# Reading roots, convolution taps, tangents and logarithms from the PSUM bank they were made in, in a twelve-sublayer kernel with five interleaved strands

## The chip, the cores and the metric

The kernel runs on one core of one Trainium2 chip. The metric is device time in microseconds (us) for one execution of the whole program; lower is better. Engines are named as the profile names them: PE is TensorE's matmuls and PEld its weight loads, DVE is VectorE, ACT is ScalarE, POOL is GpSimd, and SP is SyncE, which here only issues transfers. SBUF is the large on-chip memory. PSUM is the small one of eight banks of 128x512 f32 into which PE writes.

## The reference, cut to what matters

Eight sequences of 512 tokens with 128 channels each pass through twelve sublayers. The ones that matter here are the layer norm ahead of every sublayer and the two-directional state-space layer ("Mamba").

```python
def _layernorm(x, axis=-1, eps=1e-05):
    m = jnp.mean(x, axis=axis, keepdims=True)
    v = jnp.var(x, axis=axis, keepdims=True)
    return (x - m) / jnp.sqrt(v + eps)
...
            xz = jnp.einsum('bld,ed->ble', x, in_proj)
            xi, z = jnp.split(xz, 2, axis=-1)
...
            xc = jax.lax.conv_general_dilated(xc, conv_w, (1,), [(D_CONV - 1, 0)], dimension_numbers=('NCH', 'OIH', 'NCH'), feature_group_count=D_INNER)
            xc = xc + conv_b[None, :, None]
            xi = jax.nn.silu(jnp.transpose(xc, (0, 2, 1)))
            dbc = jnp.einsum('bld,ed->ble', xi, x_proj)
            dt, Bm, Cm = jnp.split(dbc, [DT_RANK, DT_RANK + D_STATE], axis=-1)
            dt = jax.nn.softplus(jnp.einsum('blr,dr->bld', dt, dt_w) + dt_b)
...
                h = a * h + bx
```

The state-space layer has 256 inner channels (two groups of 128, called g = 0 and 1), a causal convolution of 4 taps, and 16 states per channel. It runs once forward ("f") and once on the reversed sequence ("b"). The other sublayers are a gated feed-forward with token shift, a small gated recurrence, a capacity router, two softmax attentions with 16 heads, a 16-expert and an 8-expert mixture.

## The kernel before, in words

Data lie with channels on the partitions and the 512 tokens of one sequence ("batch" b, 0 to 7) along the free axis, so one tile is 128x512 f32. The work is cut into five strands, each a fixed sequence of jobs:

- **L** (bank PL): the first sublayers and the preparation of the attentions (jobs `ffn0`, `att0`, `l1`, `prep`).
- **M** (bank PM): the state-space layer outside its recurrence. `lnm` is its norm, `pre` the input projection, convolution, silu and softplus, `post` the gate and output projection, `fin` the closing norm.
- **S** (bank PS): the recurrence itself, 8 batches x 2 directions x 16 states = 256 steps. A step is two scans of 128x512 on DVE (line 1194, decays made by ACT in line 1487 and inputs by POOL in line 1543), a product with the output row (line 1532 on POOL for even states, line 1200 on DVE for odd ones) and an addition to the running output (line 1173).
- **F** (two banks) the mixtures and routers, **A** (three banks) the attentions (on DVE mostly the maxima of line 1115).

Every engine runs its instructions in one fixed order. `ORDER` holds for each engine a string such as `L16M1L1M10`: take 16 pieces of strand L, one of M, and so on, where a piece ends at each `yield` of the strand's generator. `weave` executes it. A semaphore per strand and engine counts finished pieces; `j.act("rs")` is the count at which ACT has made piece "rs" of job j. A waiting instruction holds up all that stand behind it on its engine.

A layer norm `ln1` is: PE centres into the bank ("cen"); ACT copies the centred values to an SBUF tile (hA or hM, line 1254) and their squares to rL or rM (line 1256); PE averages the squares into the same bank ("avg"); ACT takes Ln of the bank into rL (line 1244) and Exp of rL into rL (line 1248), which is the reciprocal root; DVE multiplies hA by rL (line 867, "h"). There are 48 such norms with hA and 8 with hM.

A job `pre` (16 in all, `mf` and `mb` of each batch) is: PE "in0" into PM, ACT copy to tM[0] (line 1320, "cp0"), PE "in1" into PM, ACT copy to tM[1] ("cp1"); DVE for both groups in turn the first tap (line 978, "c00", "c01") and the three others (line 981) from tM into du; ACT tanh of du into xi (line 1325, "si"); DVE (xi + 1) x du (line 986, "xs"); PE "xp" into PM from both groups of xi; ACT copy (line 1329, "pj"); then per group PE "dt", ACT Abs of PM (line 1334), DVE max(PM + bias, 0) into dt (line 991, "mx"), ACT Exp and Ln in tM (lines 1338, 1342), DVE dt + tM (line 996, "dt"). PE's "dt1" waits for "mx0". POOL then forms du = dt x xi (line 1518), on which the strand S of that direction waits, and DVE scales xi (line 1000).

```python
                for d in range(4):
                    for g in range(2):
                        c, x = du[p][:, g, :], tM[:, g, :]
```

Of the kernel before, what the change touches and what calls it, by code (L numbers as in the profile page):

```python
# [40 lines left out]
for _g in GROUPS:  # L41
    _at = EDGE[-1]
    for _n, _r, _c in _g:
# [18 lines left out]
    "pe": (
        "L23M1L1M1L1M1L1M1L2M1L1M1L1M2L1M1L3M3L1M2L5M1L6M1L1M1L1M2L3M1L1M1L1M2L1M1L3M3F1M1F1M1F21L1F3M1F2M1F3M1F6M1L1M1"
        "L8A1L1A2L1A1L1A2M1L1A1L3A1M1L1M1A1L1A3M3A1M1A1M1A7M2A1L1A1M1A1L1A2L1A1M1A1M1A1L1A1L1F1A1M1F1A1L1M1F3A1L1F2L1F1"
        "L1A1F2A7F1A2F2L1F1A2F2A1F1A2F2A2F1A2F2A2F1A2F2A2F1A2F2A2F1A2F2A2F3A4F2A4F1A2L1A2L1A4M1A2L1A2L1A2L1A2M1A6L1A1M1"
        "L1A1F1L1F1A1L1A1F2A1L1F1A1F2A1L1F1A1L1F2A4F1A1L1F2A1L1F1A1F2A1L1F1A1L1F2A1F1A1F2A1M1F1A1F2A1F1A1F2A1M1F2A2F1A1"
        "F1A1F1A2M1F1A1M2F1A1M1A1F1M1A1F2A1F3A1F1A2F1A1F1A2L1A3L1A2L1A2L1A2L1A2L1A2M1A1L1A5M1A2L1A4M1A10L1A18M1A5M1L1A1"
        "L1M1A1L1M1A2M1A3F1A1M1F1A1L1M1A1F2A1L1A1F1A1F1A1F1A1F1A1L1A1F1A1F1A3F1A1L1F1A1F1A1L1A1L1F1A1F1A1F1A1F1A1F1A1F2"
        "A1L1A1F2A1F1A1F6A1F2A2F1A2F2A2F2A6F1A2L1A2F1L1A2F1A14M1L1A2L1A2L1A2F2A2M1A10L1A2M1A2L1A6L1A2L1A2L1F1A1F2A1F1A1"
        "L1F2A1L1F1A1M1F2A1L1A1F1A1F2A1L1F1A1M1F2A1F1A1F2A1L1F1A1L1F2A1F1A1F2A1F2A2F1A1F1A1F1A1M1A1F1A1M2F1A1F1A4F1A1F1"  # L70
        "A1F1A1F5A1L1F1L1A1F1M1A2L1A4L1A4L1A2L1A2L1A2F1M1A14L1A2L1A8F1A4F1A12L1A2M1A2M1A2L1M1F1A1L1F2A1F2M1A1F1A1F1A1F1"
        "M1L1A1L1A2M1A1L1A3M1A1L1M1A2L1F1A1L1F1A1M1A2F2A1M1A1F1A1F1A1F1A1F1A1L1A1F2A1F1A1F2A1F1A1F2A1F1A1F2A1F1A1F2A1F4"
        "A1F2A1F1A3F2A2F1A2F2A2F2A6F1A2L1A2F1L1A2F1A10M1L2A2L1A2F2A2M1A8L1A4M1A2L1A10L1A1L1F4A1L1F2A1F1A1L1F2A1L1F1A1F2"
        "A1L1F1A1L1F2A1F1A1F2A1F1A1L1F2A1L1F1A1F2A1F2A1M1F1A1F1A1F1A1M1A2F1A1F1A1F1A2M1A1M1A1F1M1A1F1A1F1A1F1A1F1A1F1A1"
        "F1A1F1L1F1L1A1F1L1F1L1A1M1A2L1A2L1A2L1A2M1A2F1A14F1A2L1A6L1A8F1A16M1A2M1A2L1A1M1A1F1A1L1A1L1A1F1M1A1M1F3A2F1A1"
        "M1F1M1A1L1M1A1L1A3F1A1M1F1A1L1M1A1F2A2F1A1F1A1L1F1A1F1A1L1A1L1A1F2A1F1A1F2A1L1F1A1F1A1F1A1F1A1F1A1F1A1F1A1F2A1"
        "F1A1F6A1F2A2F1A2F2A2F2A6F1A2L1A2F1L1A2F1A12M1L1A2L1F2L1M1A10L1A8L1A2M1F1A2F1A2F1A2F1A2F1A1F1A1F1A1F2A2F1A1L1F2"
# [1683 lines left out]
```

## Time and profile before

| | |
|---|---|
| median of 3 runs | 3591.86 us (3588.16 to 3598.7) |
| profiled execution, its own time | 3590.76 us |
| its span, first to last instruction | 3589.0 us |
| mean granted clock of PE | 0.781 of full speed |
| busy, share of the span | PE 76%, DVE 73%, ACT 47%, POOL 47% |

The page of the profile gives busy time by engine, the chain of waits that ended last (which engine was being waited for at each moment, followed back from the end), and groups of instructions by line. "Busy" is not "late": an engine that is busy half the time may still be waited for at every step, and one that is busy three quarters of it may be waited for seldom. The span has three parts: until 124 us no scan runs, from there to about 2932 us the 256 steps of strand S run amid the rest, and after it only mixtures and attentions are left.

### The profile page before, as it was taken

To read this page: it belongs to the slowest core of one execution; us is meant where nothing else is said; L and a number is where in the kernel's file an instruction comes from. 1 tells how busy PE (TensorE), PEld (TensorE's weight loads), DVE (VectorE), ACT (ScalarE), POOL (GpSimd) and SP (SyncE) were. 2 spreads that over 40 slices of the span, in tenths; PEclk is the share of its full clock that TensorE was granted. 3 is DMA by queue.
4 is the path that set the end of the run, shared out by engine and by line. 5 is a ranking of instruction groups with operands and counts; after the bars stand their busy time and mean duration, and the time that the engine had idled before them with its cause. 6 is when DMAs were issued, how large, how long until landed. Compare 5 with 4: busy or idle time off the path is not lost.

```text
span 3589.0 us, 31663 instructions
## 1 busy us (share of the span) xinstructions
PE 2713.3 (76%) x8594; PEld 871.9 (24%) x8594; DVE 2618.9 (73%) x3818; ACT 1682.7 (47%) x2908; POOL 1696.2 (47%) x1349
## 2 busy tenths in 40 slices
PE   5405565888888887788779787888878777987887
PEld 1101122223222222223222222222222222232222
DVE  1687888878898888788878798778868775344351
ACT  3424444563636464364537373555436261532333
POOL 1486676464736465554725464556545551121101
PEclk6656566788879987798879886887679786988768
DMA  1121122131312232222312231223212220111101
GB/s 76 57 88 63 62 96 79 50 102 53 101 46 87 72 107 68 64 82 73 114 41 83 76 103 45 79 81 99 82 61 82 76 92 25 51 56 44 44 26 38
DMA packets 158881, 253.22 MB, mean 71 GB/s; under 512 B 18928, under 2 KB 56688, under 8 KB 158448
## 3 DMA queue, kind: packets, MB, share of 16 engines
q1 hardware_dynamic: 158704, 251.18, 21.8%
q8 instruction: 72, 1.18, 0.1%
q14 instruction: 105, 0.86, 0.1%
HBM read 233.81 MB, written 16.52 MB: 70 GB/s over the span
## 4 chain that ended last, share of the span: by engine, by line
PE 39%; DVE 28%; issue 11%; ACT 9%; DMA 6%; POOL 5%; SPq 3%; DVEq 0%; POOLq 0%; ACTq 0%
PE ps L466 39%; DVE rh L1194 6%; DVE nmx L1115 5%; DMA cr<-shares 4%; DVE xib L1173 3%; ACT ps L1487 2%; DVE xif L1173 2%; SPq L1642 2%; DMA Qs<-cTN 2%; ACT tN L1434 2%; POOL rb L1543 1%; POOL tF L1557 1%; DVE rh L1200 1%; DVE hA L867 1%; ACT L1231 1%
## 5 line engine op out<-in xcount | busy, mean ns | idle before, releaser
L1194 DVE TENSOR_TENSOR_SCAN rh<-ps,rb 128x512 f32<-128x512 f32 x512 | 622.9, 1217 | 105.8 <-ACT ps L1487 102.5
L1115 DVE TENSOR_REDUCE nmx<-ps 128x1 f32<-128x512 f32 (+3 forms) x1024 | 550.2, 583 | 147.9 <-PE ps L466 146.5
L1434 ACT ACTIVATE tN<-ps 128x512 f32<-128x512 f32 (+3 forms) x1024 | 473.8, 515 | 238.2 <-PE ps L466 234.8
L1532 POOL TENSOR_TENSOR rh<-rh,cs 128x512 f32<-128x512 f32 x256 | 391.1, 1532 | 378.4 <-DVE rh L1194 377.8
L466 PE MATMUL ps<-tN,strip 128*64 128x512 f32 (+3 forms) x2048 | 507.6, 574 | 10.1 <-DVE hN L1133 7.2
L466 PE MATMUL ps<-hF,W 128*128 128x512 f32 x592 | 395.4, 755 | 96.3 <-DVE tF L1055 44.4
L1543 POOL TENSOR_TENSOR rb<-duf,bs 128x512 f32<-128x512 f32 x256 | 386.4, 1527 | 115.9 <-DVE rh L1194 110.7
L466 PE MATMUL ps<-tF,W 128*128 128x512 f32 x544 | 353.5, 745 | 89.2 <-POOL tF L1557 71.1
L1543 POOL TENSOR_TENSOR rb<-dub,bs 128x512 f32<-128x512 f32 x256 | 379.1, 1500 | 76.2 <-DVE rh L1194 65.7
L1557 POOL TENSOR_TENSOR tF<-tF,cr 128x512 f32<-128x512 f32 x128 | 172.6, 1348 | 486.7 <-DMA cr<-shares 436.2
L466 PE MATMUL ps<-Ks,Qs 48*128 48x512 bf16 (+3 forms) x1024 | 291.2, 435 | 76.0 <-DVE nmx L1115 69.6
L466 PE MATMUL ps<-Qs,Ks 51*128 51x512 bf16 (+3 forms) x1024 | 231.7, 367 | 106.6 <-ACT tN L1434 52.3
L1487 ACT ACTIVATE ps<-dtb,Am 128x512 f32<-128x512 f32 x256 | 176.8, 691 | 261.5 <-DVE rh L1194 260.0
L1576 POOL COPY strip<-V 128x32 f32<-128x32 f32 x256 | 82.8, 355 | 441.9 <-PE ps L466 439.9
L1487 ACT ACTIVATE ps<-dtf,Am 128x512 f32<-128x512 f32 x256 | 177.1, 692 | 169.4 <-DVE rh L1194 168.9
L1563 POOL TENSOR_TENSOR tF<-hF,cr 128x512 f32<-128x512 f32 x128 | 177.9, 1406 | 124.2 <-DMA cr<-shares 105.0
L1369 ACT ACTIVATE tF<-ps 128x512 f32<-128x512 f32 x144 | 85.8, 596 | 312.8 <-PE ps L466 312.5
L466 PE MATMUL ps<-X,W 128*128 128x512 f32 x192 | 145.0, 855 | 96.1 <-POOL X L1510 39.6
L1173 DVE TENSOR_TENSOR xib<-xib,rh 128x1024 f32<-128x1024 f32 x128 | 198.9, 1554 | 0.3
L1173 DVE TENSOR_TENSOR xif<-xif,rh 128x1024 f32<-128x1024 f32 x128 | 194.3, 1518 | 3.7 <-POOL rh L1532 3.5
L466 PEld LDWEIGHTS ps<-Ks,Qs 48*128 48x128 bf16 x1024 | 64.6, 97 | 530.1 <-DVE nmx L1115 347.6
L466 PEld LDWEIGHTS ps<-Qs,Ks 51*128 51x128 bf16 x1024 | 63.9, 94 | 515.9 <-ACT tN L1434 286.0
(240 smaller groups left out, 3928.0 us busy)
## 6 DMA issues: line engine op xcount, KB each, us to landing
cr<-shares SPq DMA_DIRECT2D x256, 256.0 KB
bs<-rowsf SPq DMA_DIRECT2D x128, 256.0 KB, 3.6
cs<-rowsf SPq DMA_DIRECT2D x128, 256.0 KB, 3.3
bs<-rowsb SPq DMA_DIRECT2D x128, 256.0 KB, 3.7
cs<-rowsb SPq DMA_DIRECT2D x128, 256.0 KB, 3.3
parts<-spl SPq DMA_DIRECT2D x32, 384.0 KB, 2.6
Qs<-parts SPq DMA_DIRECT2D x384, 32.0 KB
Ks<-parts SPq DMA_DIRECT2D x384, 32.0 KB
```

Source lines behind the costliest of these rows:

```text
L466: return eng.matmul(o, l, r, start=start, stop=stop, skip_group_check=skip_group_check)
L1115: red(nmx[:, qt, 8 * a + i:8 * a + i + 1], PA[u % 3][:, 0:nk], AX.X, ALU.max, negate=True).then_inc(s_red, 1)
L1173: tt(xi[p][:, :, :], xi[p][:, :, :], rh[n % NH][:, :, :], ALU.add).then_inc(s_y, 1)
L1194: eng.tensor_tensor_scan(rh[n % NH][:, g, :], PS, rb[n % NBB][:, g, :], 0.0, ALU.mult, ALU.add).then_inc(s_h, 1)
L1369: act(tF[u % NG][:, :], PF[1], ACT.Tanh).then_inc(*F.by_act(j, f"si{u}"))
L1434: act(tN[e % NP][:, q0:T], PA[a][:, 0:T - q0], ACT.Exp).then_inc(s_ex, 1)
L1487: act(PS, dt[p][:, g, :], ACT.Exp, scale=Am[:, at:at + 1]).then_inc(s_a, 1)
L1532: tt(h, h, cs[n % NB][:, :], ALU.mult).then_inc(s_cp, 1)
L1543: tt(rb[n % NBB][:, g, :], du[p][:, g, :], bs[n % NB][:, :], ALU.mult).then_inc(s_bp, 1)
L1557: tt(t, t, cr[n % NC][:, :], ALU.mult).then_inc(*F.by_pool(j, f"w{i}"))
L1563: tt(t, hF[:, :], cr[n % NC][:, :], ALU.mult).then_inc(*F.by_pool(j, f"w{i}"))
L1576: eng.tensor_copy(strips[2 * (p % 2) + a][:, :, 24:32], V9[n % 2][:, :, 8 * a + 4 * g + p, :]).then_inc(s_strip, 1)
```

## The change

Four kinds of intermediate results stay in the PSUM bank in which their inputs were made, and DVE reads them there:

- the reciprocal root of `ln1` and of `fin`: ACT's Ln and Exp write PL or PM instead of rL or rM, and DVE multiplies by the bank;
- the taps: ACT's two copies per `pre` (32 in all) are gone, and DVE's four tap instructions of a group read PM;
- the tangent of `pre` is written to PM, and "xs" reads it there;
- the logarithm of `pre` is written to PM, and DVE adds it from there.

As PM is one bank, the two groups of `pre` now go one after the other: "in1" waits for "xs0" instead of "cp0"; both matmuls of "xp" wait for "xs1"; "dt1" waits for "dt0" instead of "mx0"; and ACT's Ln of group g waits for "mx". ACT's piece with the decays' constants gets a `yield` of its own. The strings of `ORDER` for all engines are new. Of these strings the diff shows one line of PE's.

```diff
-        "L23M1L1M1L1M1L1M1L2M1L1M1L1M2L1M1L3M3L1M2L5M1L6M1L1M1L1M2L3M1L1M1L1M2L1M1L3M3F1M1F1M21L1F3M1F2M1F3M1F6M1L1M1"
+        "L23M1L1M1L1M1L2M1L1M1L1M1L1M1L2M1L2M4L1M2L9M1L2M1L1M1L1M1L1M1L2M1L1M1L1M1L2M1L2M4L1F1M1F3M1F6M1F1M1F5M1F21L2M1"
...
                 for m in range(2):
                     if m:
-                        eng.wait_ge(*j.act("cp0"))
+                        eng.wait_ge(*j.dve("xs0"))
                     mm(PM, w(f"m{p}_in", m * 128, m * 128 + 128), h[:, :]).then_inc(*M.by_pe(j, f"in{m}"))
                     yield
                 for g in range(2):
-                    eng.wait_ge(*j.dve(f"xs{g}"))
+                    eng.wait_ge(*j.dve("xs1"))
...
                 for g in range(2):
                     if g:
-                        eng.wait_ge(*j.dve("mx0"))
+                        eng.wait_ge(*j.dve("dt0"))
...
-            def ln1(j, o, r):
+            def ln1(j, o, P):
                 eng.wait_ge(*j.act("rs"))
-                tt(o, o, r[:, :], ALU.mult).then_inc(*j.strand.by_dve(j, "h"))
+                tt(o, o, P, ALU.mult).then_inc(*j.strand.by_dve(j, "h"))
...
-                for d in range(4):
-                    for g in range(2):
-                        c, x = du[p][:, g, :], tM[:, g, :]
...
                 for g in range(2):
+                    c = du[p][:, g, :]
+                    eng.wait_ge(*j.pe(f"in{g}"))
+                    ts(c, PM, cw[:, 4 * g + 3:4 * g + 4], w(f"m{p}_cb", g, g + 1), ALU.mult, ALU.add).then_inc(
+                        *M.by_dve(j, f"c0{g}"))
+                    yield
+                    for d in range(1, 4):
+                        eng.wait_ge(*j.dve(f"c{d - 1}{g}"))
+                        stt(c[:, d:], PM[:, 0:T - d], cw[:, 4 * g + 3 - d:4 * g + 4 - d], c[:, d:], ALU.mult,
+                            ALU.add).then_inc(*M.by_dve(j, f"c{d}{g}"))
+                        yield
                     eng.wait_ge(*j.act(f"si{g}"))
-                    stt(xi[p][:, g, :], xi[p][:, g, :], 1.0, du[p][:, g, :], ALU.add, ALU.mult).then_inc(
-                        *M.by_dve(j, f"xs{g}"))
+                    stt(xi[p][:, g, :], PM, 1.0, c, ALU.add, ALU.mult).then_inc(*M.by_dve(j, f"xs{g}"))
...
-                    tt(dt[p][:, g, :], dt[p][:, g, :], tM[:, 1 + g, :], ALU.add).then_inc(*M.by_dve(j, f"dt{g}"))
+                    tt(dt[p][:, g, :], dt[p][:, g, :], PM, ALU.add).then_inc(*M.by_dve(j, f"dt{g}"))
...
-                act(r[:, :], r[:, :], ACT.Exp, scale=-0.5).then_inc(*k.by_act(j, rs))
+                act(r, r, ACT.Exp, scale=-0.5).then_inc(*k.by_act(j, rs))
...
-                yield from root(j, P, r, e5, "avg", "ln", "rs")
+                yield from root(j, P, P, e5, "avg", "ln", "rs")
...
             def pre(j, p):
-                for m in range(2):
-                    eng.wait_ge(*j.pe(f"in{m}"))
-                    act(tM[:, m, :], PM, ACT.Copy).then_inc(*M.by_act(j, f"cp{m}"))
-                    yield
...
-                    act(xi[p][:, g, :], du[p][:, g, :], ACT.Tanh).then_inc(
-                        *M.by_act(j, f"si{g}"))
+                    act(PM, du[p][:, g, :], ACT.Tanh).then_inc(*M.by_act(j, f"si{g}"))
...
                     eng.wait_ge(*j.act(f"ex{g}"))
-                    act(a, a, ACT.Ln, bias=one).then_inc(*M.by_act(j, f"ln{g}"))
+                    eng.wait_ge(*j.dve(f"mx{g}"))
+                    act(PM, a, ACT.Ln, bias=one).then_inc(*M.by_act(j, f"ln{g}"))
```

On DVE, at the first `pre` of the program (batch 0, forward), there stands before:

```order
L858 TENSOR_SCALAR Am<-Am 128x64
L978 TENSOR_SCALAR duf<-tM,W 128x512 x2
L981 SCALAR_TENSOR_TENSOR duf<-tM,W,duf 128x511 x2
L981 SCALAR_TENSOR_TENSOR duf<-tM,W,duf 128x510 x2
L981 SCALAR_TENSOR_TENSOR duf<-tM,W,duf 128x509 x2
L986 SCALAR_TENSOR_TENSOR xif<-xif,duf 128x512 x2
L873 SCALAR_TENSOR_TENSOR tL<-tL,ps 128x512
```

In the changed kernel DVE has at the same place:

```order
L858 TENSOR_SCALAR Am<-Am 128x64
L976 TENSOR_SCALAR duf<-ps,W 128x512
L981 SCALAR_TENSOR_TENSOR duf<-ps,W,duf 128x511
L981 SCALAR_TENSOR_TENSOR duf<-ps,W,duf 128x510
L981 SCALAR_TENSOR_TENSOR duf<-ps,W,duf 128x509
L985 SCALAR_TENSOR_TENSOR xif<-ps,duf 128x512
L976 TENSOR_SCALAR duf<-ps,W 128x512
L981 SCALAR_TENSOR_TENSOR duf<-ps,W,duf 128x511
L981 SCALAR_TENSOR_TENSOR duf<-ps,W,duf 128x510
L981 SCALAR_TENSOR_TENSOR duf<-ps,W,duf 128x509
L873 SCALAR_TENSOR_TENSOR tL<-tL,ps 128x512
```

The taps were taken in pairs, one of each group; now all four and the tangent's product ("xs0") of group 0 precede those of group 1, and `W` stands for the pointer to the tap's weights.

On PE, at the backward `pre` of batch 3, "in0" and "in1" are the rows that read `rev`, the reversed norm. `Ks,Qs` and `Qs,Ks` are scores of the attentions, `tN,strip` their values, `hF,W` and `tF,W` the mixtures. Before, one stands four rows behind the other:

```order
L466 MATMUL ps<-rM,W 128x512
L466 MATMUL ps<-Ks,Qs 128x512 x6
L466 MATMUL ps<-X,W 128x512
L466 MATMUL ps<-Ks,Qs 128x512 x2
L466 MATMUL ps<-rev,W 128x512
L466 MATMUL ps<-rF,W 128x512
L466 MATMUL ps<-Ks,Qs 128x512 x2
L466 MATMUL ps<-X,W 128x512
L466 MATMUL ps<-rev,W 128x512
```

In the changed kernel "in0" stands 72 rows ahead of "in1", of which the last ones and the rows behind it are:

```order
L466 MATMUL ps<-hF,W 128x512
L466 MATMUL ps<-tF,W 128x512
L466 MATMUL ps<-Qs,Ks 128x512 x2
L466 MATMUL ps<-tN,strip 64x512 x2
L466 MATMUL ps<-rev,W 128x512
L466 MATMUL ps<-Qs,Ks 128x512 x2
L466 MATMUL ps<-tF,W 128x512
L466 MATMUL ps<-tN,strip 64x512 x2
```

So "in1" moved behind a good part of a mixture and the end of an attention's first phase. Over the program ACT has 154 table loads in the changed order, where it had 146.

## Rows read from the trace of the kernel before

**Rows 1.** The page: span, busy time (share of the span) and instructions by engine.
```profile
span 3589.0 us, 31663 instructions
PE 2713.3 (76%) x8594; PEld 871.9 (24%) x8594; DVE 2618.9 (73%) x3818; ACT 1682.7 (47%) x2908; POOL 1696.2 (47%) x1349
```

**Rows 2.** Two windows: length, PE, PEld, DVE, ACT, POOL busy, PE's granted clock.
```profile
124.00:500.00 376.00, 153.89 (x254) 50.78 (x255) 314.45 (x307) 151.76 (x224) 266.35 (x162) 0.57 0.22 73
500.00:2932.00 2432.00, 1949.79 (x6525) 638.72 (x6523) 2008.18 (x2871) 1251.71 (x2193) 1315.57 (x1038) 0.81 0.25 78
```

**Rows 3.** The page: chain that ended last, share by engine.
```profile
PE 39%; DVE 28%; issue 11%; ACT 9%; DMA 6%; POOL 5%; SPq 3%; DVEq 0%; POOLq 0%; ACTq 0%
```

**Rows 4.** Groups by line, DVE: busy us, mean ns | idle before.
```profile
L981 DVE SCALAR_TENSOR_TENSOR dub<-tM,W,dub 128x511 f32<-128x511 f32 (+2 forms) x48 | 51.7, 1111 | 0.0
L867 DVE TENSOR_TENSOR hA<-hA,rL 128x512 f32<-128x512 f32 x48 | 51.5, 1074 | 57.8 <-ACT rL L1248 57.8
L981 DVE SCALAR_TENSOR_TENSOR duf<-tM,W,duf 128x511 f32<-128x511 f32 (+2 forms) x48 | 44.2, 969 | 0.0
L986 DVE SCALAR_TENSOR_TENSOR xif<-xif,duf 128x512 f32<-128x512 f32 x16 | 16.4, 1039 | 1.1 <-ACT xif L1325 1.1
L996 DVE TENSOR_TENSOR dtb<-dtb,tM 128x512 f32<-128x512 f32 x16 | 14.5, 906 | 2.1 <-ACT tM L1342 1.9
L996 DVE TENSOR_TENSOR dtf<-dtf,tM 128x512 f32<-128x512 f32 x16 | 13.6, 852 | 6.7 <-ACT tM L1342 6.7
L978 DVE TENSOR_SCALAR dub<-tM,W 128x512 f32<-128x512 f32 x16 | 13.3, 847 | 0.0
L978 DVE TENSOR_SCALAR duf<-tM,W 128x512 f32<-128x512 f32 x16 | 10.3, 656 | 2.6 <-ACT tM L1320 2.6
L991 DVE TENSOR_SCALAR dtf<-ps,W 128x512 f32<-128x512 f32 x16 | 11.8, 739 | 15.7 <-ACT tM L1334 15.7
```

**Rows 5.** Single lines, durations ns min/median/max, first and last start.
```profile
L867 DVE TENSOR_TENSOR hA<-hA,rL x48: 658/693/1779, 15.0 to 3372.1; 128x512 f32<-128x512 f32 x48
L862 DVE TENSOR_TENSOR hF<-ps,rF x40: 658/682/692, 405.3 to 3558.6; 128x512 f32<-128x512 f32 x40
L1532 POOL TENSOR_TENSOR rh<-rh,cs x256: 1253/1274/2419, 132.0 to 2931.0; 128x512 f32<-128x512 f32 x128
L1173 DVE TENSOR_TENSOR xif<-xif,rh x128: 1187/1218/3366, 141.0 to 2781.9; 128x1024 f32<-128x1024 f32 x128
```

**Rows 6.** Groups by line, ACT, and one of POOL: busy us, mean ns | idle before.
```profile
L1231 ACT ACT_TABLE_LOAD x145 | 186.0, 1283 | 2.5
L1320 ACT ACTIVATE tM<-ps 128x512 f32<-128x512 f32 x32 | 18.9, 592 | 12.6 <-PE ps L466 12.6
L1532 POOL TENSOR_TENSOR rh<-rh,cs 128x512 f32<-128x512 f32 x256 | 391.1, 1532 | 378.4 <-DVE rh L1194 377.8
```

**Rows 7.** Timeline of the first `pre`: start us, us, what.
```profile
103.47 0.55 DVE L978 TENSOR_SCALAR duf<-tM,W 128x512 f32<-128x512 f32 x1
111.15 1.35 DVE L986 SCALAR_TENSOR_TENSOR xif<-xif,duf 128x512 f32<-128x512 f32 x2
111.89 3.51 PE L466 MATMUL ps<-xif,W 128*96 128x512 f32 x4 [2.24 <-DVE xif L986]
119.02 1.12 PE L466 MATMUL ps<-tM,W 64*128 64x512 f32 x2 [0.32 <-DVE dtf L991]
120.91 0.69 DVE L996 TENSOR_TENSOR dtf<-dtf,tM 128x512 f32<-128x512 f32 x1 [1.94 <-ACT tM L1342]
123.67 2.34 POOL L1518 TENSOR_TENSOR duf<-dtf,xif 128x1024 f32<-128x1024 f32 x1 [9.23 <-DVE dtf L996]
```

**Rows 8.** Timeline, the second forward `pre`.
```profile
351.25 0.75 DVE L991 TENSOR_SCALAR dtf<-ps,W 128x512 f32<-128x512 f32 x1 [4.59 <-ACT tM L1334]
356.70 2.34 POOL L1518 TENSOR_TENSOR duf<-dtf,xif 128x1024 f32<-128x1024 f32 x1 [8.70 <-DVE dtf L996]
```

**Rows 9.** Waits: us in total, times, longest us.
```profile
PE ps L466 <- DVE xif L986: 15.4, 3, 12.8
```

More of the change, by code:

```diff
@@ L65 @@
[L65 to L74, printed above, removed]
@@ L192 @@
     "lnm": chain("", "rev", ln=LN1),
-    "pre": chain("in0 in1 xp dt0 dt1", "cp0 cp1 si0 si1 pj ab0 ex0 ln0 ab1 ex1 ln1",
-                 "c00 c01 c10 c11 c20 c21 c30 c31 xs0 xs1 mx0 dt0 mx1 dt1 yi0 yi1", "du", ln={}),
+    "pre": chain("in0 in1 xp dt0 dt1", "si0 si1 pj ab0 ex0 ln0 ab1 ex1 ln1",
+                 "c00 c10 c20 c30 xs0 c01 c11 c21 c31 xs1 mx0 dt0 mx1 dt1 yi0 yi1", "du", ln={}),
     "post": chain("z0 z1 o", "z0 z1 sg", "zs0 zs1", "yz", ln={}),
@@ L876, in att0 @@
             def att0(j):
-                yield from ln1(j, hA[:, PAD:], rL)
+                yield from ln1(j, hA[:, PAD:], PL)
                 eng.wait_ge(*j.act("rs2"))
-                tt(tL[:, 0, :], hA[:, PAD:], rL[:, :], ALU.mult).then_inc(*L.by_dve(j, "xn"))
+                tt(tL[:, 0, :], hA[:, PAD:], PL, ALU.mult).then_inc(*L.by_dve(j, "xn"))
                 yield
@@ L966, in lnm @@
             def lnm(j):
-                yield from ln1(j, hM[j.b % 2][:, :], rM)
+                yield from ln1(j, hM[j.b % 2][:, :], PM)
             def pre(j, p):
@@ L1092, in prep @@
                 n = ATT[j.b, l3]
-                yield from ln1(j, hA[:, PAD:], rL)
+                yield from ln1(j, hA[:, PAD:], PL)
                 qk = (("q", tL[:, 0, :], tL[:, 2, :], spl[0]), ("k", tL[:, 1, :], tL[:, 3, :], spl[1]))
@@ L1147, in strand_l @@
                     if n == "l1":
-                        yield from l1(j, PL, PL, smL, tL[:, 0, :], 0, ln1(j, hA[:, PAD:], rL))
+                        yield from l1(j, PL, PL, smL, tL[:, 0, :], 0, ln1(j, hA[:, PAD:], PL))
                     elif n in ("p2", "p3"):
@@ L1237, in ln @@
                 yield
-                yield from root(j, Bk, r, e, "avg", "ln", "rs")
+                yield from root(j, Bk, r[:, :], e, "avg", "ln", "rs")
             def root(j, Bk, r, e, avg, ln_, rs):
@@ L1243, in root @@
                 eng.wait_ge(*j.pe(avg))
-                act(r[:, :], Bk, ACT.Ln, bias=e).then_inc(*k.by_act(j, ln_))
+                act(r, Bk, ACT.Ln, bias=e).then_inc(*k.by_act(j, ln_))
                 yield
@@ L1279, in att0 @@
                 yield
-                yield from root(j, Bk, rL, e8, "avg2", "ln2", "rs2")
+                yield from root(j, Bk, Bk, e8, "avg2", "ln2", "rs2")
                 u, z, g, a = (tL[0:32, i, :] for i in (1, 2, 3, 0))
```

214 lines of the change are left out of this document (108 added, 106 removed).

## The prediction, made before the changed kernel was run

> **What bounds the kernel now.** I read the busy times first. PE is busy for 76% of the span, DVE for 73%, ACT and POOL for 47% each [rows 1]: no engine is full, and two are high. Then the windows: from 124 to 2932 us, while the scans run, DVE is busy for 314.5 + 2008.2 = 2322.7 of 2808 us, 83%, and PE for 153.9 + 1949.8 = 2103.7 us, 75% [rows 2]. So where the scans run DVE is the fullest engine, and nearly all the instructions that the change touches lie there. Third, the chain that ended last: PE holds 39% of it, DVE 28%, ACT 9%, POOL 5% [rows 3]. A microsecond of DVE work lies on that chain with a chance of about 28/73 = 0.38. These two figures, 0.38 and 0.83, are my bounds for what a microsecond taken from DVE is worth: the lower one holds if the order of everything else stayed and no second chain took over; the higher one if all engines can be packed as densely around DVE as now, its busy share unchanged.
>
> **What DVE gains.** The means and the medians of the touched lines disagree, and there the change's gain lies. The norm's product at line 867 has a median of 693 ns, but a maximum of 1779 and a mean of 1074 [rows 4, 5]. Line 862 does the same product with one operand in PSUM, 40 times through the same stretch, and never took more than 692 ns, with a median of 682 [rows 5]. An operation on two SBUF tiles is thus held up, in part of the cases for about the time of one POOL operation (median 1274 ns); one that takes a tile from PSUM is not. I price the new forms by the rows nearest to them: 0.68 us (line 862) with two tensors, 0.74 us (line 991, 739 ns) with a pointer to a weight and PSUM [rows 4]. The sum over DVE:
> - line 867 with hA: 51.5 us now, 48 x 0.68 = 32.6 then, saves 18.9 [rows 4];
> - line 981: 51.7 + 44.2 = 95.9 us now, 96 x 0.74 = 71.0 then, saves 24.9;
> - line 986: 16.4 us shown and its backward twin, equal to it, 32.8 us now, 32 x 0.68 = 21.8 then, saves 11.0;
> - line 996: 14.5 + 13.6 = 28.1 us now, 21.8 then, saves 6.3;
> - line 978: 13.3 + 10.3 = 23.6 us now, 32 x 0.74 = 23.7 then, nothing. This is a form that is cheap from SBUF when free, and its mean hides that.
>
> Together 61 us of 2619. Times 0.38 that is 23 us, times 0.83 it is 51 us. I take the middle, 0.6, or 37 us: the order was made anew, so the freed time need not stay where it falls, but PE is nearly as full.
>
> A rule of the Trainium skill speaks against these prices. First the row: two SBUF tiles 693 ns in the median, one from PSUM 682, so PSUM costs nothing more [rows 5]. The Trainium skill, "VectorE: DVE Perf Modes", in the section on the TRN2 errata, gives a fixed cost of 58 cycles from SBUF and 120 from PSUM. By that, an estimate from the page's figures, each of 264 operations would be 62 cycles or 65 ns dearer, 17 us in all, and my 37 would become 27. I go by the row.
>
> **What POOL and ACT gain.** POOL is held up by the same meetings: line 1532 has a median of 1274 ns and a mean of 1532 [rows 5, 6]. About 0.2 us on each of some 1000 products is 200 us; the touched lines make up about a fifth of DVE's time on two SBUF tiles, so some 40 us less busy, of which 5/47 lie on the chain [rows 1, 3]: 4 us. ACT loses 32 copies, 18.9 us, and gets eight more table loads (154 for 146) at 1.283, 10.3 us [rows 6]; the net of 8.6 times 9/47 is 2 us. Both bounds are near: nothing, and 8 us for both if the order makes use of them.
>
> **What the single bank costs.** In `pre` the two groups no longer overlap. At the start of the program nothing else covers this: DVE waits, and POOL's product at 123.67 us opens the first scan [rows 7]. Before, the first tap began at 103.47 and "xs1" ended at 111.15 + 1.35 = 112.50. Then: four taps 4 x 0.74, tangent 0.59 (as ACT's copy [rows 6]), "xs0" 0.68, "in1" half of 3.51 (two such matmuls took that), four taps, tangent, "xs1": 103.47 + 2.96 + 0.59 + 0.68 + 1.75 + 2.96 + 0.59 + 0.68 = 113.7, or 1.2 later. "xp" began at 111.89, 0.6 ahead of "xs1"'s end, and now can't: 0.6 more. "dt1" went to PE at 119.02 behind "mx0"; now it must await "dt0", which ended at 120.91 + 0.69 = 121.60: 2.6 more. Sum 4.4 us. The forward passage of batch 1 lies as bare: DVE sat idle 4.59 us ahead of line 991 at 351.25, and POOL 8.70 us ahead of its product at 356.70 [rows 8]. So twice, 9 us. The other fourteen I cost at nothing: they run under scans and attention of the batch in hand, DVE 83% busy. What is late next if that cover is gone is a rival below. The bounds are 4 (only the first) and 18 us (four bare passages).
>
> **Sum.** 37 + 4 + 2 - 9 = 34 us less than the profiled execution's 3590.8: 3557. The median of the runs is 1.1 above that execution, so 3558 us.
>
> **Rivals.** The bound for "no change" is 0.3%, 11 us; less than that a measurement of this kernel can't tell.
>
> *The wait only moves.* The time lost on two SBUF tiles is a wait for POOL's operation in progress. If DVE gets past the norm's product, the next operation with two SBUF tiles may meet the same POOL operation. There are 256 additions of line 1173, median 1218 ns, maximum 3366 [rows 5], which meet it already. For it: POOL is busy half the time. Against it: mostly a scan of PSUM and SBUF follows, over which POOL's operation runs out. If all moved, DVE's and POOL's terms would go and 9 - 2 = 7 us be lost: 3599, no change. By the same rule of whole operations the Trainium skill, "SBUF — State Buffer", section on port contention, has the second comer block until the first has finished; the maximum of line 867, one POOL operation above its median, agrees. Chance 0.15.
>
> *PE stands before PM.* This is the one that ends slower. PE's queue is in order. In 16 passages "in1" waited for a copy of 0.59 us and "dt1" for one DVE operation; now they wait for five DVE operations and one of ACT, and for a longer piece of the softplus. Should "in1" or "dt1" come up too soon, all the attention and mixture matmuls behind it stand, and after them the maxima and tangents. Such waits exist: three for line 986 came to 15.4 us, one of them 12.8 [rows 9]. If the 32 new ones cost 2 us each, 64 us come on top: 3622. It decides from (34 + 11)/32 = 1.4 us each. Against it: the order gives the room; at batch 3 "in1" stands 72 rows behind "in0", where it stood four behind. Chance 0.17.
>
> *The order packs better.* With 17% of DVE idle between 124 and 2932 us, the whole 61 us could come back and 10 of the idle ones with them, 34 us more than forecast: 3524. I give it 0.06, and include it in faster.
>
> **How the numbers follow.** Forecast 0.62, the wait moves 0.15, PE stands 0.17, better packing 0.06. The likeliest case alone spans, with its bounds, 51 + 8 - 4 = 55 us less (3537) to 23 - 18 = 5 less (3587). The range reaches a little past the packed side and into the two others: 3530 to 3604. A small part of the forecast falls within 11 us of before, and a small part of the moved wait outside: faster 0.67, same 0.15, slower 0.18.
>
> **What the profile after would show.** Line 867 with a mean of 680 ns and a maximum near 692; line 981 near 740 with none above 760; DVE busy 2550 to 2570 us. If the wait moves, the mean of line 1173 goes up from 1.5 us by 0.2 and DVE stays above 2600. POOL busy about 1655, ACT about 1674. The first product of POOL for the scans at 128, and that of batch 1 another 4 us later. If PE stands, waits of PE for the lines "xs" and "dt" of some 2 us times 30 are listed, and its share of the chain goes up. I would be wrong above all if the new order is worse at the places that decide, the attentions' hand-overs between PE, DVE and ACT, which no row of before can tell.

## The result, and the profile after

The changed kernel takes 3605.46 us (median of 5 runs, 3600.52 to 3611.74), the kernel before 3589.42 in the runs beside it (5 runs, 3586.83 to 3598.7). The ratio is 1.0044, with a 95% interval of 1.0025 to 1.0062: slower by some 16 us, where the prediction had it faster by 34. The profiled execution took 3605.46 us itself, its span is 3603.7.

The page of the changed kernel, its busy times and the chain that ended last, answers to [rows 1] and [rows 3]:

```profile
span 3603.7 us, 31677 instructions
PE 2720.2 (75%) x8594; PEld 881.9 (24%) x8594; DVE 2576.4 (71%) x3818; ACT 1666.1 (46%) x2884; POOL 1654.6 (46%) x1349
PE 41%; DVE 25%; issue 11%; ACT 8%; DMA 6%; POOL 5%; SPq 2%; DVEq 0%; POOLq 0%; ACTq 0%
```

Three of the four engines work less than before: DVE by 42.5 us, POOL by 41.6, ACT by 16.6. PE works 6.9 longer. The program still ends 15 us later.

The windows of the changed kernel (length, PE, PEld, DVE, ACT, POOL busy, clock), for [rows 2]:

```profile
124.00:500.00 376.00, 155.81 (x258) 51.03 (x258) 321.21 (x317) 156.27 (x228) 259.19 (x165) 0.60 0.24 77
500.00:2932.00 2432.00, 1942.84 (x6500) 646.51 (x6502) 1957.04 (x2863) 1235.87 (x2168) 1278.05 (x1034) 0.81 0.24 78
```

In the long window DVE does 51.1 us less work than before, and in the same time does 2863 instructions in place of 2871. So room was made and DVE got no further in it: it is idle for longer.

The touched lines, groups of DVE in the changed kernel (busy, mean ns of one, idle before), and two single lines (min/median/max), for [rows 4, 5]:

```profile
L981 DVE SCALAR_TENSOR_TENSOR duf<-ps,W,duf 128x511 f32<-128x511 f32 (+2 forms) x48 | 35.7, 744 | 1.3
L981 DVE SCALAR_TENSOR_TENSOR dub<-ps,W,dub 128x511 f32<-128x511 f32 (+2 forms) x48 | 35.5, 739 | 0.8
L976 DVE TENSOR_SCALAR duf<-ps,W 128x512 f32<-128x512 f32 x16 | 12.8, 798 | 4.4 <-PE ps L466 4.4
L985 DVE SCALAR_TENSOR_TENSOR xif<-ps,duf 128x512 f32<-128x512 f32 x16 | 10.8, 676 | 2.7 <-ACT ps L1319 2.6
L994 DVE TENSOR_TENSOR dtf<-dtf,ps 128x512 f32<-128x512 f32 x16 | 10.9, 679 | 9.7 <-ACT ps L1336 9.7
...
L867 DVE TENSOR_TENSOR hA<-hA,ps x48: 653/676/690, 14.7 to 3385.1; 128x512 f32<-128x512 f32 x48
L1171 DVE TENSOR_TENSOR xif<-xif,rh x128: 1186/1218/2793, 147.6 to 2764.4; 128x1024 f32<-128x1024 f32 x128
```

Every price was within 3% but one: line 867 has a mean of 32.4/48 = 0.675 us and no case above 690 ns. The additions of line 1171 keep their median of 1218 ns. No case of line 981 took more than 751 ns.

What is waited for, in the changed kernel (us in total, times, longest):

```profile
DVE rh L1192 <- ACT ps L1482: 140.2, 154, 12.1
POOL duf L1513 <- DVE dtf L994: 47.5, 3, 19.0
PE ps L466 <- DVE xif L985: 21.6, 7, 7.6
PE ps L466 <- DVE xib L985: 20.1, 3, 13.0
PE ps L466 <- DVE dtb L994: 12.2, 2, 10.8
PE ps L466 <- DVE dtf L994: 9.3, 3, 3.6
PE ps L466 <- DMA Qs<-cTN: 70.9, 12, 12.5
POOL rb L1538 <- DMA bs<-rowsb: 17.5, 3, 10.3
POOL rb L1538 <- DMA bs<-rowsf: 10.4, 2, 7.9
```

The same waits in the kernel before, where they are not in [rows 9]:

```profile
DVE rh L1194 <- ACT ps L1487: 102.5, 126, 5.9
PE ps L466 <- DMA Qs<-cTN: 51.2, 13, 10.6
POOL rb L1543 <- DMA bs<-rowsb: 5.5, 1, 5.5
POOL rb L1543 <- DMA bs<-rowsf: 4.7, 2, 4.2
```

The scans' wait for the decays is 140.2 us in 154 places, where it was 102.5 in 126; PE stands for the bank's products 63.2 us in 15 places (the four lines for 985 and 994), where it stood 18.9 for the products "xs" ([rows 9] and 3.5 more for the backward ones) and 4.7 for "mx"; PE's wait for the attentions' last operand, a transfer, rose from 51.2 to 70.9; and POOL's wait for the recurrence's rows, transfers too, from 10.2 to 27.9. Each of these could be taken for the cause, and a reader of the page alone would take one. The experiments show that the first two, waits between engines, are there in full in a kernel that gains; the last two are mostly gone in it.

### The profile page after: what moved, and what is told of

It reads as the page before. It is cut to its first block, busy times and chain, and to the rows that moved or that the text cites. A ratio compares the mean times of both kernels' runs of the same rounds, so it can differ in the third digit from the quotient of the medians.

```text
span 3603.7 us, 31677 instructions
## 1 busy us (share of the span) xinstructions
PE 2720.2 (75%) x8594; PEld 881.9 (24%) x8594; DVE 2576.4 (71%) x3818; ACT 1666.1 (46%) x2884; POOL 1654.6 (46%) x1349
## 3 DMA queue, kind: packets, MB, share of 16 engines
q1 hardware_dynamic: 158704, 251.18, 21.6%
## 4 chain that ended last, share of the span: by engine, by line
PE 41%; DVE 25%; issue 11%; ACT 8%; DMA 6%; POOL 5%; SPq 2%; DVEq 0%; POOLq 0%; ACTq 0%
PE ps L466 41%; DVE rh L1192 6%; DVE nmx L1113 5%; DMA cr<-shares 5%; DVE xib L1171 2%; ACT ps L1482 2%; DVE xif L1171 2%; SPq L1637 2%; DMA Qs<-cTN 2%; POOL tF L1552 1%; POOL rb L1538 1%; ACT tN L1428 1%; ACT L1229 1%; DVE rh L1198 1%; POOL tF L1558 1%
## 5 line engine op out<-in xcount | busy, mean ns | idle before, releaser
L1192 DVE TENSOR_TENSOR_SCAN rh<-ps,rb 128x512 f32<-128x512 f32 x512 | 622.8, 1216 | 149.8 <-ACT ps L1482 140.2
L1527 POOL TENSOR_TENSOR rh<-rh,cs 128x512 f32<-128x512 f32 x256 | 375.1, 1468 | 447.4 <-DVE rh L1192 447.2
L1538 POOL TENSOR_TENSOR rb<-dub,bs 128x512 f32<-128x512 f32 x256 | 360.8, 1428 | 102.5 <-DVE rh L1192 84.7
L466 PE MATMUL ps<-tF,W 128*128 128x512 f32 x544 | 338.1, 715 | 83.6 <-POOL tF L1552 65.4
L466 PE MATMUL ps<-Qs,Ks 51*128 51x512 bf16 (+3 forms) x1024 | 227.7, 369 | 124.2 <-DMA Qs<-cTN 70.9
L1571 POOL COPY strip<-V 128x32 f32<-128x32 f32 x256 | 92.2, 392 | 394.3 <-PE ps L466 382.7
L466 PE MATMUL ps<-X,W 128*128 128x512 f32 x192 | 153.3, 900 | 89.4 <-POOL X L1505 32.4
L1198 DVE TENSOR_TENSOR rh<-rh,cs 128x1024 f32<-128x1024 f32 x128 | 189.7, 1482 | 7.3
```

The lines of the kernel that those rows point to most:

```text
L466: return eng.matmul(o, l, r, start=start, stop=stop, skip_group_check=skip_group_check)
L1192: eng.tensor_tensor_scan(rh[n % NH][:, g, :], PS, rb[n % NBB][:, g, :], 0.0, ALU.mult, ALU.add).then_inc(s_h, 1)
L1198: tt(rh[n % NH][:, :, :], rh[n % NH][:, :, :], cs[n % NB][:, :].unsqueeze(1).broadcast_to([128, 2, T]), ALU.mult).then_inc(s_cv, 1)
L1527: tt(h, h, cs[n % NB][:, :], ALU.mult).then_inc(s_cp, 1)
L1538: tt(rb[n % NBB][:, g, :], du[p][:, g, :], bs[n % NB][:, :], ALU.mult).then_inc(s_bp, 1)
```

## The experiments

All kernels compute the whole reference. Times are medians, with the ratio to the kernel before and its 95% interval.

| kernel | us | ratio |
|---|---|---|
| changed kernel | 3605.46 | 1.0044 (1.0025 to 1.0062) |
| roots alone, old order | 3571.93 | 0.9941 (0.9921 to 0.9961) |
| changed, roots in SBUF | 3602.37 | 1.0027 (1.0014 to 1.004) |
| changed, logarithms in SBUF | 3600.73 | 1.0017 (1.0003 to 1.0032) |
| new order, all edits undone | 3698.27 | 1.029 (1.0273 to 1.0307) |
| before, other order of transfers | 3623.86 | 1.008 (1.0063 to 1.0098) |
| changed, other order of transfers | 3585.84 | 0.9978 (0.996 to 0.9997) |
| roots alone, other order of transfers | 3595.17 | 1.0006 (0.9993 to 1.002) |
| before, loads in halves | 3450.52 | 0.9602 (0.9581 to 0.9623) |
| changed, loads in halves | 3428.46 | 0.9541 (0.9522 to 0.956) |
| roots alone, loads in halves | 3431.33 | 0.9551 (0.9523 to 0.9578) |
| changed, roots in SBUF, loads in halves | 3438.96 | 0.9554 (0.9524 to 0.9585) |
| new order, all edits undone, loads in halves | 3549.72 | 0.9883 (0.9862 to 0.9904) |

**The roots alone, in the order of before.** The norm's Ln and Exp write the bank and DVE multiplies by it; everything else, the strings of `ORDER` too, is as before.

```diff
-            def ln1(j, o, r):
+            def ln1(j, o, P):
                 eng.wait_ge(*j.act("rs"))
-                tt(o, o, r[:, :], ALU.mult).then_inc(*j.strand.by_dve(j, "h"))
+                tt(o, o, P, ALU.mult).then_inc(*j.strand.by_dve(j, "h"))
...
-                yield from root(j, P, r, e5, "avg", "ln", "rs")
+                yield from root(j, P, P, e5, "avg", "ln", "rs")
```

> The kernel before, in its own order, with the roots alone in the bank (norms, the second root of the recurrence, the closing norm); taps, tangents and logarithms stay as before. Line 867's 48 products should fall from 1074 to about 680 ns, 19 us less DVE, the same as in the changed kernel. Theory A (the changed kernel's loss comes from the single-bank passage of the projection: in1 behind xs0, dt1 behind dt0): this one has none of that, so 7 to 16 us faster than before (19 us times 0.38 to 0.83). Theory B (the loss is in the order made anew, whatever the edits): the same 7 to 16 us faster, as the order is the old one. Theory C (a wait taken from one DVE instruction goes to the next one with two SBUF tiles): within 4 us of before, and the mean of line 1173 up.

It took 3571.93 us, 21 less than the kernel before in the runs beside it. That is more than the 7 to 16 us of theories A and B, and far from theory C's 4. DVE is busy 2600.0 us, 18.9 less than before, and that is just what the prediction had for line 867. Put down to DVE alone, a microsecond off it at the norm was worth a whole one, more than either of my bounds; but POOL was busy 16.6 us less as well, and the run doesn't tell the two shares apart. One of the four edits, made in the old order, beats both kernels.

**The changed kernel without the roots, and without the logarithms.** The new order stays, and one edit is undone in each.

```diff
-                yield from root(j, P, P, e5, "avg", "ln", "rs")
+                yield from root(j, P, r[:, :], e5, "avg", "ln", "rs")
```

```diff
-                        eng.wait_ge(*j.dve("dt0"))
+                        eng.wait_ge(*j.dve("mx0"))
...
-                    eng.wait_ge(*j.dve(f"mx{g}"))
-                    act(PM, a, ACT.Ln, bias=one).then_inc(*M.by_act(j, f"ln{g}"))
+                    act(a, a, ACT.Ln, bias=one).then_inc(*M.by_act(j, f"ln{g}"))
```

> The changed kernel in its new order, with the roots back in SBUF. Theories A and B: the 19 us of DVE come back, 7 to 16 us slower than the changed kernel, 3612 to 3622. Theory C: within 4 us of the changed kernel.

> The changed kernel in its new order, with the logarithms back in SBUF and dt1 waiting for mx0 again. 6 us of DVE time come back (line 994, 32 additions). Theory A: the waits of PE and POOL behind dt0 go (PE 21 us, POOL 47 us in three waits listed after the change), so 5 to 12 us faster than the changed kernel, the start 2.6 us earlier. Theory B: the order is unchanged and made for the later dt1, so within 4 us, the start alone earlier by 2.6.

They took 3602.37 and 3600.73 us. Under the new order the roots, worth 21 us in the old, show no worth: without them the kernel is 3 us faster by the medians and 6 by the ratios, though DVE is busy 2592.9 us in it, 16.5 more. The logarithms in the bank cost 5 us by the medians and 10 by the ratios (the two groups of runs stand beside different runs of the kernel before), which lies between the two theories. The hand-overs at the bank that the logarithms add may therefore hold 5 to 10 of the 16 us. They are no explanation of the 50 that are missing against the forecast.

**The new order alone.** All edits are undone, while the strings of SyncE, PE and POOL are those of the changed kernel. ACT copies the projection again, at places where it was waiting anyway; its string is changed for that in many places, and DVE's in one.

```diff
-                        eng.wait_ge(*j.dve("xs0"))
+                        eng.wait_ge(*j.act("cp0"))
...
+                    eng.wait_ge(*j.pe(f"in{g}"))
+                    act(tM[:, g, :], PM, ACT.Copy).then_inc(*M.by_act(j, f"cp{g}"))
+                    yield
...
-                    c = du[p][:, g, :]
-                    eng.wait_ge(*j.pe(f"in{g}"))
+                    c, x = du[p][:, g, :], tM[:, g, :]
+                    eng.wait_ge(*j.act(f"cp{g}"))
```

> The new order with all four edits undone: roots and logarithms are read from SBUF again, the taps and tangents from SBUF, ACT's 32 copies of the projection are back (put in where ACT waits anyway), and both groups of a state-space input job stay one after the other, since the new order wants them so; the strings of SyncE, PE and POOL are those of the changed kernel. It tells what the order alone costs. Theory 'the order': the order itself loses more than the edits bring; the edits are worth about 20 us as the roots alone were in the old order, so this kernel should be the changed one plus about 20 us, 3625 (3615 to 3640), and by comparison with the kernel before the new order as such costs 35 us. Theory 'the bank': what loses are the hand-overs of the single bank, which this kernel mostly doesn't have; then it should take 3575 to 3600. If the edits are worth nothing under the new order, as the roots (3 us faster without them) and the logarithms (5 us faster) suggest, it will lie at 3600 to 3610.

It took 3698.27 us, 93 more than the changed kernel and 107 more than the runs of before beside it. All three expectations missed. The new order is of no use without its edits. How much of the 93 us is the longer DVE work, how much the copies and the places that I gave them, this kernel does not tell. So it shows that this order needs its edits, and not what the order by itself costs.

**SyncE's order alone.** SyncE issues all transfers in one queue. In three kernels its string alone was replaced: the attentions' splits stand about three places later, the mixtures' shares about one earlier. No engine computes anything in another order. The first pieces of the string, in the kernel before:

```diff
-        "M1S17M1S47M1S27F4S4F3S1F1M1F1S14P1S1P2S1P1S3P1S2P1S11M1S13A1S6F6S4F2S2F1S7M1S3P1S2P5S2F4S2F2S2F3S4F1S1F3S1F3A1"
+        "M1S22M1S42M1S26F1S2F3S2F3S2F1M1S4F1S10P2S1P2S15P2S2M1S12A1S3F1S1F2S3F1S1F2S3F1S1F2S7M1S2P1S1P4S2F1S2F1S2F3S1P1F3S"
```

> The kernel before with one string of its order changed, SyncE's: the transfers that split the attentions' operands go on average 3.3 places later in its queue, those of the mixtures' shares 1.3 places earlier; 545 of 938 pieces move by at least one place (mostly by less than 10, those of the attentions by up to 16). No engine computes anything else or in another order. Theory 'the queue': POOL waits 541 us for the shares (436 + 105) and the queue's issues of such transfers take 4 to 12 us where transfers of the recurrence's rows take 0.4, so the time is decided by which transfer stands behind which; then this should save 20 us or more, 3570 or less. Theory 'the transfers are covered': DMA holds 6% of the chain and SyncE's queue 3%, and which transfer goes first changes nothing by more than 11 us: 3580 to 3600.

> The changed kernel with SyncE's string alone changed in the same manner as in the kernel before (attention's splits 3.2 places later on average, the mixtures' shares 1.2 earlier). If the changed kernel's loss is a matter of its queue of transfers, it becomes as fast as, or faster than, the kernel before treated in the same way: below 3580 here, and within 5 us of it. If the loss lies with the waits among PE, DVE and ACT, it stays 15 us or more behind the kernel before so treated.

> The old order with the roots in the bank (3572 us so far), and SyncE's string changed in the same manner (attention's splits 2.5 places later on average, the mixtures' shares 1.1 earlier). If the two gains are independent, it stands 21 us below the kernel before so treated; if the queue decides, the roots' 21 us are worth less here. If the queue's order is covered, 3565 to 3580.

None of the sizes that I had set came out; the three went apart: the kernel before lost 32 us (3623.86), the roots alone lost 23 (3595.17), the changed kernel gained 20 (3585.84). My hope of a better order for all was wrong. Between the kernels so treated, the roots alone stand 29 us ahead of the kernel before, and the changed kernel stands 38 ahead, not 16 behind. Each string was made for its own kernel, so this is no clean comparison. But the sizes speak: moving transfers by a few places in a queue that computes nothing moves the time by 20 to 32 us in either direction, more than the change under study did. The theory that the transfers are covered falls. What this queue is doing is seen in its timeline. SyncE in the kernel before, from 1188 to 1222 us (start us, us, what):

```profile
1188.80 14.75 SPq L1660 DMA_DIRECT2D cr<-shares  x5
1204.29 4.74 SPq L1610 DMA_DIRECT2D cs<-rowsb  x1
1209.07 0.55 SPq L1606 DMA_DIRECT2D bs<-rowsb  x1
1209.66 11.26 SPq L1660 DMA_DIRECT2D cr<-shares  x3
1220.96 5.19 SPq L1610 DMA_DIRECT2D cs<-rowsb  x1
```

And the transfers of the same kernel from 1190 to 1204 us, in 40 slices: the busy share of the 16 DMA engines in tenths, and what they moved:

```profile
DMA  5211111111111113111111111111111111111111
GB/s 181 100 47 53 53 53 47 53 53 53 47 53 47 35 23 82 23 47 53 53 47 53 53 53 53 47 53 53 47 47 53 47 53 47 47 53 47 47 53 47
```

An issue of the recurrence's rows takes 0.32 or 0.43 us in the median. Here five loads `cr` take 14.75, and a transfer for the recurrence that stands behind them takes 4.74 just to be issued. While the loads `cr` of that mixture run, the DMA engines move some 50 GB/s with between one and two tenths of their time busy, so one load of 256 KB works out at 5.2 us; elsewhere in the program the same queue reaches 200 to 400 GB/s. These 128 loads (16 jobs of 8, all of the 16-expert mixture) spread two rows over 64 partitions each, and their source is written with an outer dimension of 2. The Trainium skill, "DMA: Bandwidth & Descriptors", in the section on why a DMA increments its semaphore by 16, says that a transfer is split over as many engines, up to 16, as divide its slowest dimension on both sides; for a dimension of 2 these would be two. The trace agrees: two of 16 would be busy for an eighth of the engines' time, and the slices while these loads run show the digit 1.

**The loads in halves.** So the next edit issues each of the 128 loads as two transfers of 64 partitions: the same bytes, at the same place of every order.

```diff
-                            src = (shares[2 * i - 2:2 * i, :].unsqueeze(1).broadcast_to([2, 64, T]) if two
-                                   else shares[i - 1:i, :].broadcast_to([128, T]))
-                            dma(cr[m % NC][:, :], src).then_inc(s_cr[m % NC], 16)
+                            if two:
+                                for a in range(2):
+                                    dma(cr[m % NC][64 * a:64 * a + 64, :], shares[2 * i - 2 + a:2 * i - 1 + a, :]
+                                        .broadcast_to([64, T])).then_inc(s_cr[m % NC], 16)
+                            else:
+                                dma(cr[m % NC][:, :], shares[i - 1:i, :].broadcast_to([128, T])).then_inc(
+                                    s_cr[m % NC], 16)
```

> The kernel before, with only the transfers of the first mixture's shares changed: each of the 128 loads that spread two rows over 64 partitions each is issued as two transfers of 64 partitions (128 KB) in place of one of 128; the same bytes, the same places in every order. In the kernel before, such a load moves at about 50 GB/s with 1 to 2 of 16 DMA engines busy, so it takes 5.2 us, and the transfers behind it in SyncE's queue (issues of 5.2 us) and POOL at line 1557 (436 us of waits) stand for it. Theory 'the queue': if the two transfers are spread over all engines, as the one-row loads of 256 KB are, they take 1.6 us or less together; POOL's wait at line 1557 falls from 436 to below 250 us and the time by 40 to 120 us: 3470 to 3550. Theory 'covered': the transfers are hidden by other work, 3580 to 3600.

> The changed kernel with the same edit. Theory 'the queue', by which the changed kernel loses its gain in SyncE's queue and the transfers behind it (it became 20 us faster when that queue alone was reordered): the difference to the kernel before with the same edit goes from +16 us to -5 or below. Theory 'the order among PE, DVE and ACT': the difference stays at +10 to +25 us, or grows, since the transfers no longer cover the stands at the single bank.

> The old order with the roots in the bank (3572 us so far) with the same edit. If the two gains are independent, 21 us below the kernel before with that edit, and the fastest kernel of the study; if the roots' gain came by way of the queue, less than 10 us below it.

The kernel before takes 3450.52 us with it, 143 less. The changed kernel takes 3428.46, and is now 22 us faster than the kernel before, not 16 slower: the intervals of the two ratios, 0.9522 to 0.956 and 0.9581 to 0.9623, don't meet. The roots alone take 3431.33, 19 us below the kernel before with halves, so their gain is independent of the transfers in the old order. In the kernel before with halves SyncE issues ten halves in 10.21 us, and the transfers behind them without delay:

```profile
1158.83 10.21 SPq L1663 DMA_DIRECT2D cr<-shares  x10
1169.78 0.33 SPq L1613 DMA_DIRECT2D cs<-rowsb  x1
1170.15 0.43 SPq L1609 DMA_DIRECT2D bs<-rowsb  x1
```

While they run, more of the engines move more. The transfers of that kernel from 1158 to 1172 us, in 40 slices:

```profile
DMA  4045557665656575620045632000000015744689
GB/s 88 29 181 181 141 76 275 211 181 141 246 170 211 187 299 170 193 94 18 29 176 193 217 111 70 0 0 0 0 0 0 0 70 193 281 164 82 164 164 199
```

The changed kernel with halves: busy times, the chain that ended last, and waits (us in total, times, longest):

```profile
PE 2661.1 (78%) x8594; PEld 867.1 (25%) x8594; DVE 2579.5 (75%) x3818; ACT 1666.8 (49%) x2884; POOL 1657.1 (48%) x1349
PE 48%; DVE 29%; issue 9%; ACT 9%; POOL 3%; DMA 1%; SPq 0%; DVEq 0%; POOLq 0%; ACTq 0%
...
PE ps L469 <- DVE xif L988: 21.4, 6, 6.7
PE ps L469 <- DVE xib L988: 20.1, 3, 13.0
PE ps L469 <- DVE dtb L997: 12.2, 2, 10.8
PE ps L469 <- DVE dtf L997: 9.4, 3, 3.7
```

Transfers and SyncE fell from 8% of the chain to 1%. The four waits of PE at the bank come to 63.1 us in 14 places, where they were 63.2 in 15 in the changed kernel that lost. They are there in a kernel that gains 22 us: they are not what turned a gain into a loss. What they cost in both kernels, no run tells. The scans' wait for the decays stays too: 123.5 us, where the kernel before has 90.6 with halves. The waits for transfers don't. In the two kernels with halves, before and changed, they are:

```profile
PE ps L469 <- DMA Qs<-cTN: 10.2, 7, 4.0
PE ps L469 <- DMA Qs<-cTN: 10.6, 6, 4.0
POOL rb L1541 <- DMA bs<-rowsb: 6.9, 3, 4.3
```

The third line is the changed kernel's; POOL waits for no rows in the kernel before with halves. With the slow loads these waits of the changed kernel stood 20 and 18 us above those of the kernel before, and with halves 0 and 7. So the growth of 37 us in the waits for transfers that stand behind the slow loads shrinks to 7, while the growth at the bank and at the decays stays.

**What hid the roots and the edits.** Two kernels of the new order, with the loads in halves.

> The changed kernel without the roots in the bank (3602 us with the slow transfers, 3 us less than the changed kernel), now with the loads of the first mixture's shares issued in two halves as in the run that took 3428 us. If the slow transfers are what made the roots worth nothing, the roots are worth 15 to 22 us again, so this takes 3443 to 3450. If the roots are worth nothing in this order for another reason (a wait of PE at a full bank, say), it takes 3424 to 3434.

> The new order with all four edits undone and ACT's copies back (3698 us with the slow transfers, 93 more than the changed kernel), with the loads in two halves. If the 93 us are inherent in giving this order longer DVE instructions and 32 more hand-overs by copies, it stays 80 to 100 us above the 3428 of the changed kernel with halves: 3508 to 3528. If most of them came by way of the slow transfers, it is less than 60 above: below 3488. Either way it tells the new order as such from the edits: the kernel before with halves took 3451.

Without the roots the changed order takes 3438.96 us with halves, 10.5 more than with them. With the slow loads it had been 3 us less with them gone. This lies between the two expectations. But the runs of this kernel scatter more than others (3413.69 to 3443.87), and the intervals of the two ratios, 0.9524 to 0.9585 without the roots and 0.9522 to 0.956 with them, cover each other. So it is not shown that the slow loads hid the roots' worth, nor that the roots have any in this order. With all edits undone it took 3549.72, 121 above the changed kernel with halves, more than the 80 to 100 that I had expected and more than the 93 with the slow loads. What the edits bring within their own order is larger once the transfers are fast.

The five pairs side by side show what the slow loads cost each: 143 us before, 141 with the roots alone, 149 in the new order with the edits undone, 163 with the roots undone, 177 in the changed kernel. In the new order the cost grows with the DVE time that the edits save; the step from 149 to 163 and 177 rests in part on the scattered runs. The timeline shows the places, in one execution of each kernel. In the kernels with slow loads, DVE's last product of the state-space layers (line 1020 after, 1022 before) begins at 2957.8 us after and 2954.3 before, and the rest takes 645.9 after and 634.7 before; with halves it begins at 2825.8 and 2838.7, and the rest takes 602.9 and 608.8. So of the 33.5 us between the two comparisons of the profiled spans (plus 14.7, minus 18.8) 16 come in the stretch of the scans and 17 in the tail, where only mixtures and attentions run. In that tail of the changed kernel POOL's waits for the loads at line 1552 are 183.2 us, of the kernel before 173.2 (line 1557). Over the whole program, and with line 1558 (before 1563) counted in, they are the same, 541.9 and 541.2 us: POOL does not wait longer for the loads themselves. While the scans run it is the waits for the transfers behind the loads that grew, the attentions' operand from 39.8 to 56.8 us and the recurrence's rows from 10.2 to 27.9.

## Why the prediction was wrong

**The sum over DVE** had the right mechanism. Lines 867, 981, 985 and 994 came to 32.4, 71.2, 21.6 and 21.7 us, where I had 32.6, 71.0, 21.8 and 21.8. One price was off: the first tap (line 976) takes 0.80 us from the bank, not 0.74, 2 us in all. The total of DVE fell by 42.5 us, not 61; besides those 2, operations that the change doesn't touch took up some 17 again. The scaling of xi in the forward direction (line 998) went from 13.7 to 18.5 us, the products of line 1198 from 183.4 to 189.7. So a part of the waits did move, over a quarter of what the rival "the wait only moves" would have had, though not to the place it named: the additions of line 1171 came to 393.5 us in both directions, where they were 393.2. Line 998 reads a single SBUF tile, so "two SBUF tiles" in the prediction was too narrow: its forward operations have a median of 1480 ns, where they had 559.

The rule on fixed costs (the Trainium skill, "VectorE: DVE Perf Modes", TRN2 errata) would, by an estimate from its figures, have made each of these operations 65 ns dearer from the bank. Line 867 is 17 ns cheaper in the median (676 for 693). Only the first tap went the way of the rule, and further: its median is 799 ns from the bank, where it was 538 from SBUF (forward direction).

**POOL and ACT** came as told: POOL fell to 1654.6 us (told 1655), ACT to 1666.1 (told 1674). 153 table loads are in the trace, for 154.

**The single bank at the start** cost more than my 4.4 us. The first product of POOL for the scans begins at 130.89 us, where it began at 123.67, so 7.2 later. The timeline of the changed kernel shows the hand-overs that I had left out:

```profile
108.86 0.69 DVE L985 SCALAR_TENSOR_TENSOR xif<-ps,duf 128x512 f32<-128x512 f32 x1 [1.39 <-ACT ps L1319]
109.61 1.12 PE L466 MATMUL ps<-hM,W 128*128 128x512 f32 x2 [1.32 <-DVE xif L985]
110.78 0.81 DVE L976 TENSOR_SCALAR duf<-ps,W 128x512 f32<-128x512 f32 x1 [1.22 <-PE ps L466]
115.35 3.73 PE L466 MATMUL ps<-xif,W 128*96 128x512 f32 x4 [3.75 <-DVE xif L985]
122.50 0.75 DVE L989 TENSOR_SCALAR dtf<-ps,W 128x512 f32<-128x512 f32 x1 [7.21 <-ACT tM L1327]
125.74 0.69 DVE L994 TENSOR_TENSOR dtf<-dtf,ps 128x512 f32<-128x512 f32 x1 [2.49 <-ACT ps L1336]
130.12 0.69 DVE L994 TENSOR_TENSOR dtf<-dtf,ps 128x512 f32<-128x512 f32 x1 [0.82 <-ACT ps L1336]
```

"xs1" ended at 114.60 + 0.69 = 115.3 us, not at 113.7, and between "dt0" and "dt1" lie 130.12 - 125.74 = 4.38 us, since the whole softplus of the second group (its matmul, Abs, max, Exp and Ln) now stands behind the first's. I had counted only the later start of one matmul. As to the second bare passage, the product of batch 1 came no later than before, at 356.63 us for 356.70. So the term's 9 us came to some 7 by luck: one passage dearer than told, the other at nothing.

**The rival "PE stands"** was a good description of the waits and not of what decided. PE stands 63.2 us for these lines, some 40 more than before, close to the 45 us from which by my own bound it decides. But the same waits are in the kernel that gains 22 us. The row of waits shows that an engine stood, not that the end stood with it.

**The step that failed** is the one that turned DVE's time into the end's: "I take the middle, 0.6, or 37 us: the order was made anew, so the freed time need not stay where it falls". It priced the order's use of the freed time without asking for a resource outside the four engines. The chain showed DMA at 6% and SyncE's queue at 3%, and I read past both. Its factor of 0.6, bounded by 0.38 and 0.83, measured 1.1 in the old order (21 us for 18.9) and below nothing in the new one; with the loads in halves DVE works 44.9 us less than in the kernel before with halves (2579.5 for 2624.4), and the changed kernel gains 22 us, of 34 that the sum gave. With the slow loads it loses 16. The forecast would have been off by 12 us rather than 47 in a kernel without the slow loads. The size of DVE's term, 61 us for a measured 42.5, was wrong too, but 0.6 of 42.5 is still 25 us of gain and turns no sign.

**What stays open.** That the transfers decide the sign is shown: with the loads in halves and nothing else changed, a loss of 16 us becomes a gain of 22. It holds for the order of the transfers as it was. With another order of them the slow loads stayed and the changed kernel still stood 38 us ahead of the kernel before, so the loss needs both the slow loads and their place in the queue. By which hand-over it comes about is not shown. The waits that grew with the slow loads and not with halves, for the attentions' operand and the recurrence's rows, are the nearest; but their sums don't follow the time from one order of transfers to the next. In the other order they are 137.6 us in the kernel before, which lost 32 us by it, and 133.1 in the changed kernel, which gained 20. Nor was it tried to give the taps and tangents in the bank the old order, in which two groups of a job overlap; so 22 us are the worth of the edits with their order, and the roots alone in the old order have 19 of them: what taps, tangents and logarithms add beside a new order is 3 us, which these runs can't tell from nothing.

## What to carry to other kernels

Before pricing what a microsecond of an engine is worth, look at the queue of transfers for issues that take many times their usual length, and at the rate while they run: a broadcast at 50 GB/s with one to two tenths of the DMA engines' time busy is a bound outside the engines' busy times, and here repairing it was worth 143 us where the change under study moved 16. A reordered program is a new program: time the smallest edit in the old order first, since it may keep the whole gain (21 us here) that the new order loses. And test a suspected wait by finding a kernel that has it and is fast; the 63 us of PE's waits at the bank stood in the kernel with the lowest median too.
